# Attention stage of a graph network on VectorE: four multiply-and-accumulates per item, or one multiplication and one tensor_reduce

## The reference: what is computed

```
Q = x @ Wq;  K = x @ Wk;  V = x @ Wv
e = jnp.sum(Q[receiver] * K[sender], axis=-1) * scale      # one dot product of 128 numbers per edge
m = segment_max(e, receiver);  w = exp(e - m[receiver])
denom = segment_sum(w, receiver);  numer = segment_sum(w[:, None] * V[sender], receiver)
x + where(denom > 0, numer / denom, 0) @ Wo
```

## Time and profile before

| what | value |
|---|---|
| runs | 5154.44, 5148.17, 5146.24 us; median 5148.17 us |
| the profiled execution | span 5144.9 us from the first to the last instruction; the page gives no other time for it, and the three runs lie 1.3 to 9.5 us above this span |
| instructions | 72170, of which VectorE 11785 |
| busy over the whole span | PE 62%, PEld 47%, DVE 66%, ACT 56%, POOL 71% |
| mean granted TensorE clock | 0.767 |
| mean DMA rate | 168 GB/s |

### The profile page before, as it was taken

One profiled execution on the slowest core, in us unless ns is written; L12 is line 12 of the kernel. 1 busy time (PEld: TensorE's weight loads), 2 busy tenths in 40 slices (PEclk: granted clock), 3 DMA queues, 4 the chain that ended last, 5 costly groups with the idle time before them and its releaser, 6 DMA issues. The chain is left out here.

```text
span 5144.9 us, 72170 instructions
## 1 busy us (share of the span) xinstructions
PE 3166.0 (62%) x15758; PEld 2414.5 (47%) x15758; DVE 3394.4 (66%) x11785; ACT 2871.6 (56%) x7156; POOL 3664.3 (71%) x3635
## 2 busy tenths in 40 slices
PE   3555555545652666166476746666988887777774
PEld 3554555523431444155465634544555465555552
DVE  6587566658886777467499973333777776666664
ACT  0114666638874888268367762333555566666663
POOL 5777777767774777378677717776777677777777
PEclk9655555569996888689689978888555599989887
DMA  2336888858872777356478858887677632222222
GB/s 72 78 80 197 250 251 255 251 126 249 251 232 76 226 229 225 96 166 203 133 207 222 222 171 235 225 224 202 197 206 205 180 74 73 72 72 71 71 73 60
DMA packets 820080, 862.65 MB, mean 168 GB/s; under 512 B 161384, under 2 KB 595149, under 8 KB 819227
## 3 DMA queue, kind: packets, MB, share of 16 engines
q1 hardware_dynamic: 703656, 673.59, 42.6%
q0 software_dynamic: 112896, 179.36, 15.5%
q10 hardware_dynamic: 3314, 7.36, 0.4%
HBM read 494.63 MB, written 370.82 MB: 168 GB/s over the span
## 5 line engine op out<-in xcount | busy, mean ns | idle before, releaser
L1929 POOL DMA_INDIRECT gs_xs<-t_t,kept_idx_b x392 | 370.0, 944 | 228.4 <-issue 118.9
L1035 POOL DMA_INDIRECT t_alpha<-gsm_raw,gsm_edge_idx x392 | 386.2, 985 | 165.6 <-issue 117.0
L2193 POOL DMA_INDIRECT mss_xs<-t_x,kept_idx_a x392 | 387.8, 989 | 144.2 <-issue 118.5
L2049 POOL DMA_INDIRECT gs_xs<-t_z,kept_idx_a x392 | 384.5, 981 | 138.3 <-issue 119.2
L2185 POOL DMA_INDIRECT out_dram<-mss_o,kept_scat_idx x392 | 394.9, 1007 | 119.4 <-issue 117.9
L1227 PE MATMUL gsm_hp<-kept_w,gsm_zT 128*128 128x128 f32 x1568 | 252.5, 309 | 357.9 <-ACT gsm_zT L1093 357.5
L1025 POOL DMA_INDIRECT gsm_raw<-t_al,kept_idx_b x392 | 379.0, 967 | 124.5 <-issue 118.5
L1598 POOL DMA_INDIRECT att_xs<-t_t,kept_idx_a x392 | 371.5, 948 | 134.2 <-issue 117.3
L536 POOL DMA_INDIRECT sort_xs<-in_x_dram,kept_src_idx x392 | 379.8, 969 | 119.5 <-issue 119.5
L534 POOL DMA_INDIRECT sort_xd<-in_x_dram,kept_dst_idx x392 | 378.7, 966 | 119.4 <-issue 119.4
L216 PE MATMUL gs_tp<-kept_ident,gs_xs 128*128 128x128 f32 x784 | 277.5, 370 | 263.6 <-DMA gs_xs<-t_t,kept_idx_b 154.6
(11 more groups left out here) (556 smaller groups left out, 11014.5 us busy)
## 6 DMA issues: line engine op xcount, KB each, us to landing
t_t<-sort_o SPq DMA_DIRECT2D x61, 858.0 KB
t_x<-gsm_o SPq DMA_DIRECT2D x196, 264.0 KB
sort_x<-in_x_dram SPq DMA_DIRECT2D x61, 832.0 KB
gsm_x<-t_t SPq DMA_DIRECT2D x196, 256.0 KB
t_z<-gsm_z SPq DMA_DIRECT2D x196, 256.0 KB
out_dram<-gsm_o SPq DMA_DIRECT2D x196, 256.0 KB, 3.1
t_t<-l_o SPq DMA_DIRECT2D x49, 528.0 KB, 3.1
att_own<-t_t SPq DMA_DIRECT2D x98, 264.0 KB
```

What stands on the lines that cost most here:

```text
L1035: pool.indirect_dma_start(T["alpha"], bass.IndirectOffsetOnAxis(edge_idx[:, c:c + 1], 0), raw[:, c, :], None).then_inc(scattered[u], 16)
L1929: pool.indirect_dma_start(xs[u][:, j, :], None, T["t12"], bass.IndirectOffsetOnAxis(K["idx_b"][:, c:c + 1], 0)).then_inc(gathered[u], 16)
L2049: pool.indirect_dma_start(xs[u][:, j, :], None, T["z1"], bass.IndirectOffsetOnAxis(K["idx_a"][:, c:c + 1], 0)).then_inc(gathered[u], 16)
L2193: pool.indirect_dma_start(xs[q % BUFS][:, j, :], None, T["x3"], bass.IndirectOffsetOnAxis(K["idx_a"][:, c:c + 1], 0)).then_inc(gathered[q ...
```

## The change: what it does

`dot` becomes one `tensor_tensor` over the item's whole 128 x 512 tile, from `qp` in PSUM and the gathered rows in SBUF into `prod` in SBUF. A new part, `sum_dot`, stands directly behind it in the same slot: it waits for `dotted`, and one `tensor_reduce` sums `prod` (seen as 128 x 4 x 128) along its last axis into the item's four columns of `block_dots`. It raises a new semaphore, `dot_summed`, for which `scale_dots` now waits. `dotted`, for which TensorE's `multiply` waits, is now raised by the multiplication.

```diff
-        chain_v, o_set = sem("chain_v"), sem("o_set")
+        chain_v, o_set, dot_summed = sem("chain_v"), sem("o_set"), sem("dot_summed")
...
             def dot(q):
                 dve.wait_ge(multiplied, q + 1)
                 dve.wait_ge(gathered[q % RING], 64 * (q // RING) + 64)
-                for j in range(4):
-                    place = 4 * (q % BLOCK) + j
-                    dt = dve.tensor_tensor_reduce(prod[q % 2][:, j, :], qp[q % 2][:, j, :], xs[:, q % RING, j, 0:D], 1.0, 0.0, ALU.mult, ALU.add,
-                                                  block_dots[q // BLOCK % 2][:, place:place + 1])
-                dt.then_inc(dotted, 1)
+                dve.tensor_tensor(prod[q % 2][:], qp[q % 2][:], xs[:, q % RING, :, 0:D], ALU.mult).then_inc(dotted, 1)
+
+            def sum_dot(q):
+                place = 4 * (q % BLOCK)
+                dve.wait_ge(dotted, q + 1)
+                dve.tensor_reduce(block_dots[q // BLOCK % 2][:, place:place + 4], prod[q % 2][:], mybir.AxisListType.X, ALU.add).then_inc(dot_summed, 1)
 
             def scale_dots(b):
-                dve.wait_ge(dotted, BLOCK * (b + 1))
+                dve.wait_ge(dot_summed, BLOCK * (b + 1))
...
-            in_slots((dot, 2, 1, ITEMS), (scale_dots, FIRST_STEP, BLOCK, BLOCKS),
+            in_slots((dot, 2, 1, ITEMS), (sum_dot, 2, 1, ITEMS), (scale_dots, FIRST_STEP, BLOCK, BLOCKS),
```

## The result

The changed kernel takes **5178.29 us** in the median of four runs (5177.77 to 5179.40), against 5147.24 for the kernel before in the same comparison: a ratio of **1.0063, 95% interval 1.0051 to 1.0075**, 31 us slower. The forecast was 5185.3 in a range of 5163 to 5209. The profiled execution of the changed kernel has a span of 5176.4 us, 31.5 more than the 5144.9 of before.

A forecast was written before the change was run, and what follows sets the result against it. VectorE's stream bounds the attention stage from item 20: 38.2 us for 78 items, +0.13 early, -1.5 for exponents, +0.3 for block ends, sum +37.1 on 5144.9; with 3.3 from span to median 5185.3 us, range 5163 to 5209.

The forecast's parts named there:

- What bounds the stage: Attention stage: from item 20 to the end VectorE's own stream is the path, so its dots' cost moves the stage's end.
- The early waits: VectorE's waits for gathers ahead of item 16, 3.4 us each in the mean, hide a change of half a microsecond.
- The pair's price: VectorE, per item: multiplication 0.73 plus reduction 0.60 is 1.33 us against 0.84 for the old instructions, +0.49 us.
- Behind a block's last item: VectorE at block ends: the pair costs 1.46 us against the old 0.94, +0.52, adding 0.3 us for 11 blocks.
- The three waits for exponents: VectorE's three waits for ScalarE's exponents each shrink by 0.49 us, -1.5 us in all.
- Ahead of item 20: Waits for gathers absorb the extra of items 16 to 19 except for 0.13 us.
- 78 items x 0.49: Items 20 to 97 on VectorE each cost 0.49 us more, 38.2 us in all.
- GpSimd is held: GpSimd waits some 24 us for ScalarE's weighting; its last gather starts near 2990 instead of 2966, at no cost.
- rival C: TensorE's granted clock falls with longer slots; fully at 0.5 the stage is 97 us longer, 5245 us; chance 5%.
- A: VectorE's stream: durations count, saving 0.05 or 0.31 us an item, 5144 or 5130 us; chance 4% no change, 3% faster.
- B: VectorE's reduction costs 0.35 us (5166 us in all) or 1.19 (5229 us); chance 4% towards low, 6% towards high.
- the rule that the prediction named as speaking for the change: Trainium skill, VectorE: small tiles pay a fixed latency each time, tiles of 512 elements or more amortise it; table estimate +17 us.

The follow-up runs named there:

- 3: Only items 0 to 15 in the new form, the others as in the kernel before: 5145.54 us, ratio to before 1.0002.
- 4: Only items 59 to 97 in the new form, the others as in the kernel before: 5162.92 us, ratio to before 1.0032.
- 2: The changed kernel with every item's reduction made twice, the first time into a spare tile: 5218.94 us, ratio to before 1.0143.
- 9: The kernel before with ScalarE's exponents ahead of its root and apply in the slot: 5132.26 us, ratio to before 0.9981.
- 6: The kernel before with one dot product of four for each item, the other three left out: 5127.56 us, ratio to before 0.9962.
- 5: The changed kernel with TensorE's multiply waiting for the reduction instead of the multiplication, releasing PSUM later: 5182.28 us, ratio to before 1.0067.
- experiment 1: The changed kernel with the older item's count moved between the multiplication and the reduction: 5163.33 us, ratio to before 1.0039.

## Why the prediction was right, and by how much it was off

**What bounds the stage.** Right. VectorE's stream is the path from item 18 or 20 on: only late items count (3, 4), and what is added or taken there comes out nearly in full (2, 9) until the gathers' floor is met (6). The early waits hid what they were said to hide.

**The pair's price.** Right in kind, a little high. Said were 0.73 + 0.60 against 0.84, +0.49; measured in the mean over the stretch 0.708 + 0.604 against 0.842, +0.470. The reduction, for which the trace had no row, has the distance of the nearest pass, 0.604 where 0.60 was taken. There was some luck in that: the rows bounded it only by 0.35 and 1.19, and nothing in them showed that a reduction would go like the `tensor_tensor` of rows 7. The distance behind the multiplication was put 0.02 too high: the operation of rows 6 lasts 0.70 us, this one 0.66 to 0.69, and the dependent start comes 0.03 behind the end in both. Behind a block's last item 1.43 against 0.955, +0.475 where 0.52 was said. Over 77 intervals that is 36.2 us instead of 37.7.

**What was left out.** The multiplication starts on the average 0.01 to 0.02 us sooner behind the work ahead of it than the old instruction did (0.10 against 0.12 behind `scale`), about 1 us. The three waits for exponents shrank from 2.66 to 2.22, and a fourth of 0.18 came: -1.2 instead of -1.5. Together 36.2 - 1.0 - 1.2 = 34.0 us, where 32.6 were measured between items 20 and 97. The last 1.4 us are shorter distances between the softmax's small steps, the largest 0.40 us in the 11 starts behind `att_row_unjoined`; what shortens them wasn't tested, and it may be scatter. Ahead of item 20 the stage lost nothing and was 0.8 us quicker against its own start (said: +0.13), within the 2 us by which this part differs from kernel to kernel. Behind item 97 it is 0.5 us longer, the last dots themselves.

**The sum.** +37.1 was said, the stage gave +32.2, the span +31.5. Of the 4.9 us between, the term "78 items x 0.49", with its 0.3 for the block ends 38.5 us, accounts for 1.8: it measured 36.2 + 0.5 = 36.7, some 5% less. The rest are effects that the sum put at nothing or nearly so: 1.0 for the multiplication's sooner start, 1.4 in the softmax's steps and 1.0 ahead of item 20, less 0.3 for the exponents. The median was 7.0 us under the forecast of 5185.3: 5.6 of them from the span, and 1.4 since the 3.3 us carried over from span to median were 1.9 here. The pair's price is read from 77 distances and is a firm correction; each of the other pieces is no larger than what two executions of the same stages differ by.

**The other engines.** GpSimd is held for 25.3 us (24 said) and issues its last gather at 2987.8 (2990 said), at no cost. TensorE's granted clock did fall, from 0.91 to 0.84 over the stretch, as rival C had it, but VectorE waited for nothing of TensorE's there, which agrees with rival C's own price: even at 0.59 an item's matmuls were put at 5.5 us, under a slot of 5.74. The semaphore raised earlier is worth nothing that shows (5).

**The rivals.** A, durations: refuted by experiments 1 and 2 and by the result's sign. B, another price of the reduction: refuted, 0.604. The Trainium skill (VectorE: DVE Perf Modes, The perf-mode tier table) has tensor_reduce in the 1x mode only; by estimate, at one element a cycle of that page's 0.96 GHz clock, 512 elements are 0.53 us, and the measured distance, 0.604, lies above that. The table of fixed costs in the Trainium skill (the same page, the section on the TRN2 errata), from which the prediction estimated +17 us, had the right sign; the measured old price, 0.84 where it gives 1.03, is most of what separates it from the 32, and the new pair's 1.31, where it gives 1.25, the rest. So the rule that the prediction named as speaking for the change spoke, by its own table, against it.

## What to carry to other kernels

Price instructions on one busy engine by the distance from one start to the next, taken from the order of time, and not by their mean duration: four fused multiply-and-accumulates of 128 elements are 0.84 us of a busy VectorE though they add up to 1.44, and the two wide instructions that touch the data twice are 1.31 though they add up to 1.36. A product with its sum right behind it on the same engine costs 0.11 us more than one with other work between. And once an engine's stream is the path, look at its last remaining waits before its arithmetic: moving one small operation up in ScalarE's order gave 8 to 9 us, where no other way to make all four dot products gained anything that shows.

## What the runs showed of the hardware that was not expected

- A reduction that doesn't stand right behind its producer was itself a little shorter, 0.587 us to the next start instead of 0.604 (experiment 1), and the second of two reductions in a row has 675 ns of length instead of 686 (experiment 2). Why wasn't tested.
- ScalarE's sum of 128 elements is two instructions, of 302 and 189 ns, about 0.30 us from start to start, so it is dearer than VectorE's whole multiply-and-accumulate at 0.21.

```profile
L1750 ACT ACTIVATE att_dump<-att_prod x196: 292/303/314, 2490.0 to 2992.4; 128x128 f32<-128x128 f32 x196
L1750 ACT ACTIVATION_READ_ACCUMULATOR att_dump<-att_prod x196: 185/189/197, 2490.2 to 2992.6; 128x1 f32 x196
```

- The granted clock of TensorE fell with the longer slots (0.91, 0.84 and, with two reductions, 0.81 between its two levels) although TensorE's busy time in the stretch rose, from 281.5 to 308.2 us. The number of matmuls recorded is nearly the same, 1977 and 1984, so one took 0.155 us in the mean instead of 0.142, about as much more as the clock is lower.
